# The residual added on TensorE and copied by ScalarE, in place of VectorE's addition

## The reference, cut to what matters

```python
def layer(x):                                   # x: 4 x 32 x 32 x 64, fp32
    z = layer_norm(layer_norm_c(x))             # per token, over 64 channels
    y = mamba(z)                                # in_proj, conv, silu, selective scan with 16 states, gate, out_proj
    y = layer_norm(y + skip_scale * z)
    x = x + (y @ proj_w.T + proj_b)             # <- the residual of this case
    t = tokens(x)                               # 4096 tokens
    return t + moe(layer_norm(t))               # router with capacity, 8 experts 64 -> 256 -> 64
```

## The kernel before, in words

| n | TensorE | ScalarE | VectorE |
|---|---|---|---|
| 4, 5 | back: transposes of n2 onto bank M1 (L843) | back (n = 5, 6): M1 to bT (L603) | |
| 6 | back: projection bT x PW onto M1 (L848), signals b_pr | | |
| 7 | | front: Silu of u and sz (L529, L532), with a table load before (L529) and after (L504) | back: rows = M1 + x (L1113), waits for b_pr, signals b_t1 |
| 8, 9 | front: rows of B and C onto M1 / M0 (L796), back: transposes of the rows onto M1 (L857), waits for b_t1 | front: M to bcs (L539), back: M1 to bT (L607) | |
| 9, 10 | front: delta's projection (L805), waits for bcs | | |
| 10, 11 | back: centring of the rows (L865) | front (L549, L550, L556, L559), back: sq and cg (L612, L613), signals b_cg | |
| 12 | back: logits (L872) | front (L562 to L566) | back: variance (L1117), waits for b_cg |
| 13 | | back: inverse root (L581, L583), signals b_rs3, and the rows (L622) | back: router (L1122 on), waits for b_rs3 |

## Time and profile before

### The profile page before, as it was taken

One profiled execution on the slowest core, in us unless ns is written; L12 is line 12 of the kernel. 1 busy time (PEld: TensorE's weight loads), 2 busy tenths in 40 slices (PEclk: granted clock), 3 DMA queues, 4 the chain that ended last, 5 costly groups with the idle time before them and its releaser, 6 DMA issues. The chain is left out here.

```text
span 423.6 us, 4314 instructions
## 1 busy us (share of the span) xinstructions
PE 334.6 (79%) x1293; PEld 191.7 (45%) x1293; DVE 327.0 (77%) x356; ACT 223.7 (53%) x392; POOL 257.5 (61%) x196
## 2 busy tenths in 40 slices
PE   7914997657999847599984877896987699999980
PEld 3312432225544423544442354452443568788860
DVE  4799979999999979999887996999596126435541
ACT  5456576906757781655778145455251255544420
POOL 2527746793665686697567678468766203665572
PEclk9965899978799998679998869887598569999995
DMA  5197999998778965778872257877880720000000
GB/s 106 21 336 225 283 299 414 284 324 306 248 274 266 320 220 157 221 265 308 266 282 79 80 172 193 265 214 190 214 250 6 203 58 5 4 23 11 15 5 13
DMA packets 44306, 78.60 MB, mean 186 GB/s; under 512 B 16419, under 2 KB 22339, under 8 KB 44282
## 3 DMA queue, kind: packets, MB, share of 16 engines
q1 hardware_dynamic: 41450, 73.88, 55.7%
q0 software_dynamic: 2832, 4.44, 3.6%
HBM read 72.30 MB, written 7.41 MB: 188 GB/s over the span
## 5 line engine op out<-in xcount | busy, mean ns | idle before, releaser
L433 POOL TENSOR_TENSOR prod<-h,csb 128x1024 f32<-128x1024 f32 (+1 forms) x80 | 155.1, 1946 | 79.7 <-DVE h L1086 50.9
L816 PE MATMUL Yp<-prod,ident 128*128 128x512 f32 x256 | 142.5, 683 | 33.9 <-POOL prod L433 33.9
L1086 DVE TENSOR_TENSOR_SCAN h<-dA,Bp 128x1024 f32<-128x1024 f32 (+1 forms) x64 | 128.7, 2015 | 4.0 <-POOL prod L433 0.6
L573 ACT ACTIVATE dA<-delta,aneg 128x1024 f32<-128x1024 f32 (+1 forms) x80 | 76.7, 971 | 51.1 <-DVE delta L1055 24.5
L816 PEld LDWEIGHTS Yp<-prod,ident 128*128 128x128 f32 x256 | 50.3, 215 | 95.7 <-POOL prod L433 52.5
L1064 DVE TENSOR_TENSOR Bp<-Cp,bsb 128x1024 f32<-128x1024 f32 x48 | 59.1, 1232 | 3.6 <-DMA bsb<-bc_rows 2.0
L492 POOL DMA_INDIRECT out_dram<-dA,h x20 | 20.0, 1002 | 33.3 <-DVE dA L1253 28.4
L463 POOL DMA_INDIRECT slots<-rows_,slot x28 | 29.4, 1049 | 7.7 <-issue 6.2
L1071 DVE TENSOR_TENSOR Bp<-Cp,bsb 128x1024 f32<-128x1024 f32 x16 | 19.7, 1233 | 8.1 <-DMA bsb<-bc_rows 6.8
L1239 DVE TENSOR_TENSOR dA<-Bp,b2s 128x320 f32<-128x320 f32 x8 | 3.9, 491 | 25.4 <-PE Bp L979 25.4
L1086 DVE TENSOR_TENSOR_SCAN h<-dA,hl,Bp 128x512 f32<-128x512 f32 x16 | 20.1, 1273 | 2.4 <-POOL prod L433 1.7
(11 more groups left out here) (249 smaller groups left out, 518.6 us busy)
## 6 DMA issues: line engine op xcount, KB each, us to landing
bsb<-bc_rows SPq DMA_DIRECT2D x48, 512.0 KB, 5.5
csb<-bc_rows SPq DMA_DIRECT2D x48, 512.0 KB, 5.7
bsb<-bc_rows SPq DMA_DIRECT2D x32, 256.0 KB, 4.6
csb<-bc_rows SPq DMA_DIRECT2D x32, 256.0 KB, 4.1
slots<-fill POOLq DMA_DIRECT2D x1, 2600.0 KB, 22.7
h<-slots SPq DMA_DIRECT2D x4, 325.0 KB, 4.2
csb<-slots SPq DMA_DIRECT2D x3, 325.0 KB, 5.8
xs_in<-in_x_dram SPq DMA_DIRECT2D x1, 768.0 KB, 5.5
```

Source lines behind the costliest of these rows:

```text
L433: po.tensor_tensor(prod[:, k % 4, c], h[:, k % 3, c], csb[:, k % CSLOTS, c], ALU.mult).then_inc(s_pP, 1)
L573: ac.activation(dA[:, k % 3, c], delta[:, c], ACT.Exp, scale=aneg[:, n:n + 1]).then_inc(s_dA, 1)
L816: ins = te_.matmul(Yp[:, HB[q]], idn, prod[:, k % 4, HB[q]], start=False, stop=(n == 15), skip_group_check=True)
L1086: ve.tensor_tensor_scan(h[:, k % 3, c], dA[:, k % 3, c], Bp[:, :] if whole else Bp[:, HB[n % 2]], hl[:, n:n + 1] if v == CARRY + 1 else 0. ...
```

## The change

VectorE's addition of the residual (L1113) goes. In its place TensorE adds x onto the projection's bank M1 with one more matmul, of the unit matrix `idn` (128 x 128) times x (128 x 512 fp32 for a whole unit, 128 x 256 for a half), in the same accumulation group; b_pr is signalled by that one. ScalarE copies M1 to the rows in turn 7, with the waits that VectorE had, and signals b_t1. On ScalarE `back` of turn 7 stands ahead of `front` of turn 7, so the copy stands ahead of the Silus.

```diff
@@ scalar, back(v, n)
+                if n == 7:
+                    act.wait_ge(b_pr, v + 1)
+                    if v >= 2:
+                        act.wait_ge(b_sent, sent(v - 1))
+                        act.wait_ge(b_res, 16 * (v - 1))
+                    ac.activation(rows(v)[:, 0:nt, R_RES:R_RES + C], tiles(M1[:, 0:nt * C], C, nt), ACT.Copy).then_inc(b_t1, 1)
@@ tensor, back(v, n)
                 if n == 6:
                     pe.wait_ge(b_n2T, quads(v + 1))
                     for t in range(nt):
-                        ins = te_.matmul(M1[:, t * C:(t + 1) * C], bT[:, t * P:(t + 1) * P], PW[:, :], start=True, stop=True)
-                    ins.then_inc(b_pr, 1)
+                        te_.matmul(M1[:, t * C:(t + 1) * C], bT[:, t * P:(t + 1) * P], PW[:, :], start=(t == 0),
+                                   stop=False, skip_group_check=True)
+                    te_.matmul(M1[:, 0:nt * C], idn, xs_in[:, b, t0:t0 + nt, :].rearrange("p t c -> p (t c)"), start=False,
+                               stop=True, skip_group_check=True).then_inc(b_pr, 1)
@@ vector, back(v, n)
-                if n == 7:
-                    dve.wait_ge(b_pr, v + 1)
-                    if v >= 2:
-                        dve.wait_ge(b_sent, sent(v - 1))
-                        dve.wait_ge(b_res, 16 * (v - 1))
-                    ve.tensor_tensor(rows(v)[:, 0:nt, R_RES:R_RES + C], tiles(M1[:, 0:nt * C], C, nt),
-                                     xs_in[:, b, t0:t0 + nt, :], ALU.add).then_inc(b_t1, 1)
```

## The result

The changed kernel takes 430.2 us (median of 14 runs, 427.57 to 436.44) against 426.7 for the kernel before (14 runs, 423.56 to 429.14): a ratio of 1.0086, 95% interval 1.0046 to 1.0125. That is 3.5 us slower by the medians, and by the interval between 2.0 and 5.3 us. Ratios here leave out the executions in the core's slower state, which medians and ranges include, and the profiled executions of e1, e3, e9 and e11 fell in that state. The profiled execution took 428.02 us, with a span of 426.3 (before 425.27 and 423.6).

What follows compares the result with a forecast made beforehand. It took ScalarE to set when VectorE goes on in turn 13 of units 1 and 2. 2 x 1.74 - 0.31 + 0 + 0.80 = +3.97 us on 427.07 gave 431.0 us, range 426.6 to 433.3.

Steps and rivals of the forecast that it cites:

- The 2.71 of the wait: Loop of unit 1, turn 7: ScalarE's first table load starts 2.71 us later behind the copy, 2.1 of it pure waiting.
- 1.74 per loop: Loops of units 1 and 2: the second L539 starts 1.74 us late, and VectorE goes on in turn 13 that much later.
- The slack of 0.97: Ahead of the second L539 in units 1 and 2: the part of ScalarE's 2.71 us delay that is absorbed, 0.97 us.
- TensorE's own 0.86: Loops of units 1 and 2: the added matmul's 0.86 us alone would hold the second L539 if the Silus started earlier.
- Unit 2: Loop of unit 2: same pattern as unit 1, another 1.74 us; VectorE's gains are given back in turns 12 and 13.
- Unit 3: Loop of unit 3, no front: the scan starts earlier without the addition, a gain of 0.31 us, bounds 0 and 0.68.
- Unit 4: Loop of unit 4: gain between 0 and 0.41 us, taken as 0; the extra matmul, uncovered, would cost up to 0.86.
- The last back: Last back, on the chain of waits: 0.86 us for the matmul, -0.06 for copy against addition; +0.80, bounds 0.37 and 0.86.
- (a): Rival, loops: table load runs ahead of the copy, each loop costs about 0.86 us; +2.2 in all, 429.3; chance 0.15.
- (b): Rival, loops: ScalarE catches up before turn 13, given over 2.7 us of idle time; -3.2 us, 423.9; chance 0.13.
- (c): Rival, whole kernel: slack takes most of the 2.7 us, VectorE's head start the rest; about 427.3 us; chance 0.12.
- (d): Rival, loops: nothing absorbs the 2.71 us and unit 4's extra matmul shows; +7.1 us, 434.1; chance 0.10.

Runs made afterwards that it cites:

- e1: Changed kernel with ScalarE's copy behind turn 7's Silus and table loads in the loops; ratio to the kernel before 1.0026, in a second run 1.0089.
- e3: Changed kernel without the added matmul, so the residual is left out; ScalarE still copies ahead of the Silus; ratio to the kernel before 0.9979.
- e9: Kernel before with only a wait of ScalarE for the projection added in turn 7, ahead of the Silus; ratio to the kernel before 1.0052.
- e11: e8 with the change made in the back of unit 2 alone (loop of unit 3); ratio to the kernel before 0.9924.
- e5: Kernel before with the change in the backs of units 0 and 1 alone (loops of units 1 and 2); 430.24 us against 426.89, ratio 1.0085.
- e6: Kernel before with the change in the backs of units 2, 3 and 4 alone; ratio to the kernel before 1.0003.
- e2: Changed kernel with VectorE, not ScalarE, copying the bank where its addition stood; ratio to the kernel before 1.0151, in a second run 1.0119.
- e4: Changed kernel with the Silu table loaded ahead of the copy in turn 7 of the loops of units 1 and 2; ratio to the kernel before 1.0147.
- e8: Kernel before with ScalarE's inverse root for the router moved ahead of the front's piece of turn 12; 423.79 us, ratio to the kernel before 0.9907.

## Why the prediction was right

**What bounds: right, but for the turn.** VectorE's head start was given back, and ScalarE's lateness at the second L539 reached the router undiminished (1.87 there, 1.96 and 1.85 at the router). It met VectorE in turn 12, though, at the variance, for ScalarE's cg, and not in turn 13. The prediction named two signs for this that don't agree: a wait in turn 13 that grows "or is split with the one at the variance", and "wrong if VectorE's wait in turn 13 doesn't grow". That wait was 2.4 and 2.5 and stayed at 2.5, so by the second sign the forecast failed. The sign was badly chosen: cg stands behind the same late second L539 as the root, so VectorE meets the lateness at cg first. The variance comes 24.22 us after the projection's start in place of 22.41, 1.81 late, and the way from there to the router is about as long as before (6.69 for 6.54). e5 and e6 place the loss: +2.2 to +5.1 us with the change in the loops of units 1 and 2 alone, -1.3 to +1.6 with the rest alone.

**The 2.71 of the wait: 2.85.** The copy took 0.60, not 0.58, it started 0.04 behind the matmul's end, and the load began 0.06 behind the copy's end. So 1.74 per loop was 1.87 at the second L539, and 1.85 to 1.96 at the router.

**The slack of 0.97: right (0.98).** e9, e3 and the changed kernel put 1.32, 1.93 and 2.85 us of delay on the table load and get 0.33, 0.95 and 1.87 at the second L539: each time 0.98 or 0.99 less. The slack is shown by these rows.

**TensorE's own 0.86 under it: right.** e1, e2 and e4 take ScalarE's lateness off in three ways and all stop at +0.85 at the second L539. Their totals don't show it: by the ratios they are +1.1 and +3.9 us for e1, +6.6 and +5.2 for e2 and +6.5 for e4, where +2.0 to +2.5 was expected and the changed kernel has +3.7. So that another place of the copy saves time in all is not shown. The changed kernel's 1.87 is that the copy waits for the matmul: ScalarE's part alone is 0.95, the matmul adds 0.92 to it.

**Unit 2: the step was right, the stage not.** The stage grew by 0.80, not 1.74. From the projection on it lost its 1.87; ahead of it TensorE had caught up. The rows of the diagonal's matmul, before and after:
```profile
181.16 3.73 PE L812 MATMUL Yp<-u,diagD 128*128 128x512 f32 x4
```
```profile
182.55 2.97 PE L818 MATMUL Yp<-u,diagD 128*128 128x512 f32 x4
```
The granted clock was 0.50 over these rows before and 0.65 in the changed kernel. What was 1.39 late at the gate was 0.33 late at the projection. e5, with the same change in these loops, has 73.03 and 73.11, +2.23 and +1.16 on the one profile of before, and e6, without it, +1.47 and -1.07, so such shifts are of an execution rather than of the change.

**Unit 3: -0.59 for -0.31**, inside the bounds. The scan moved up by 0.30, as written; besides, the wait for the transfer of B was 3.17 for 3.66. **Unit 4: +0.28 for 0**, inside the bounds: TensorE's later logits (L880) held the router for 0.2. **The last back: +0.92 for +0.80.** The added matmul was 0.97, not 0.86; the granted clock was 0.50 from the projection's start to the matmul's end, and 0.50 over the projection before, so a matmul more did not lift it.

**The sum** of the steps was +3.97; the profiled spans differ by 2.7 and the medians by 3.5. The steps as measured (2 x 1.9 - 0.6 + 0.3 + 0.9 = 4.4) lie above both; the rest is what TensorE caught up ahead of the projections (1.1 in unit 2, 0.2 in unit 1) and 0.4 ahead of the first gate. That the forecast came within half a microsecond of the medians is in part luck: the steps were 0.4 too small together, the total is known to 1.7 us either way, and it alone doesn't exclude the +2.2 of (a). The rows do.

**The rivals.** (a) was a true mechanism but not this kernel's: the load did stand behind the copy, and e4, which moves it ahead, gives just (a)'s 0.86 at the second L539. (b) fails at its own point: 0.98 us of slack where over 2.7 were needed. (c) is excluded by the interval, which begins at +2.0 us; the slack took 0.98 of the 2.85, not most of it. (d) fails on the slack as well: it wanted none. The rule of the Trainium skill ("ScalarE: Activation LUTs", section "Rules for kernel authors") gives such work to VectorE as faster per element, with a figure for bf16; no run here has this copy or this addition in bf16, and for this fp32 bank the rows say otherwise: 0.60 for the copy, 0.68 for the addition and, in e2, 0.68 for VectorE's plain copy.

## What to carry to other kernels

Before moving work to the engine with the lower busy share, look at the place in its queue: what stands behind the new instruction, and whether its input is ready when the engine gets there. Here a copy of 0.6 us cost 2.85 of ScalarE's time because it waited 2.25 first, and the chain behind it had 0.98 us of slack. And read the busiest engine's few pauses first: two of 2.5 us, each of which waited for two short instructions of ScalarE, were worth 3.1 to 4.0 us (e8), while the 0.68 us of work taken off VectorE in each of these loops was waited away. Last, read a change's effect between rows that repeat, not from a stage of one profile.

## What the runs showed of the hardware

In the two sessions where all kernels stood higher, the experts' stage took 59 to 65 us in every profile in place of 53.54. VectorE's largest wait there, in e1's second run:
```profile
DVE dA L1240 <- remote: 26.2, 3, 9.2
```
What released it is nothing that the profile shows. The 26.2 are not all extra: before, VectorE waited 25.4 us at this line, eight times, at most 4.3 us each, for TensorE. TensorE, busy without a pause from 350 to 404 us before, was busy for 58.3 of the 63 us from 352 to 415 here. No profile of the other two sessions, before and after among them, has such a line. It is not the change, since e9 and e11, which have nothing of it in the last back and the experts, took 65.07 and 62.12. Nor is it the chip alone, since the last session ran on the same one as e5 to e8. What it was stays open.
